# Where the update's weight chunks are split: GpSimd's early share ends four chunks sooner

## The reference

```python
def _L0_gnn_ref(n_f, ...):
    feat = jnp.concatenate([n_f[edge_src], n_f[edge_dst]], axis=1)
    e_hh = relu(feat[:E_HH] @ W_hh + b_hh)          # 128 edges
    e_oo = relu(feat[E_HH:E_HH + E_OO] @ W_oo + b_oo)   # 640 edges
    e_ho = relu(feat[E_HH + E_OO:] @ W_ho + b_ho)       # the rest
    logit = (concatenate([e_hh, e_oo, e_ho]) @ W_a + b_a)[:, 0]
    alpha = softmax of logit over the edges with the same edge_dst
    z_f = segment_sum(alpha[:, None] * n_f[edge_src], edge_dst)
    nf2 = jnp.concatenate([n_f, z_f], axis=1)
    h_new = relu(nf2[:64] @ W_hn + b_hn)
    o_new = relu(nf2[64:] @ W_on + b_on)
    return jnp.concatenate([h_new, o_new])
x = layernorm(x + L0(x, ...)); x = layernorm(x + L1(x, W, a, src, dst))
```

## Time and profile before

| what | value |
|---|---|
| three runs, median | 407.93 us (407.68 to 408.96) |
| profiled execution | 406.15 us |
| its span, first to last instruction | 404.2 us |
| mean granted TensorE clock | 0.924 |
| TensorE busy | 329.3 us, 81% of the span |
| VectorE, ScalarE, GpSimd busy | 303.8, 190.3, 142.5 us |

### The profile page before, as it was taken

One profiled execution on the slowest core, in us unless ns is written; L12 is line 12 of the kernel. 1 busy time (PEld: TensorE's weight loads), 2 busy tenths in 40 slices (PEclk: granted clock), 3 DMA queues, 4 the chain that ended last, 5 costly groups with the idle time before them and its releaser, 6 DMA issues.

```text
span 404.2 us, 4665 instructions
## 1 busy us (share of the span) xinstructions
PE 329.3 (81%) x1434; PEld 254.9 (63%) x1434; DVE 303.8 (75%) x398; ACT 190.3 (47%) x287; POOL 142.5 (35%) x202
## 2 busy tenths in 40 slices
PE   1889999991899769699999999972899990699480
PEld 1668888870355558488888888741688880588330
DVE  1599999933718958699999999898567689715635
ACT  3364585200302324786768777425246673323233
POOL 3200080460200710058988977392004332007000
PEclk9989999997799989899999999997799997589886
DMA  7995689799199955000300300333446982000002
GB/s 241 411 404 204 233 303 325 250 275 271 29 373 361 318 202 208 2 0 2 105 2 2 105 2 2 83 125 104 161 152 210 344 296 86 0 0 2 1 0 104
DMA packets 17639, 63.63 MB, mean 157 GB/s; under 512 B 2234, under 2 KB 2236, under 8 KB 17360
## 3 DMA queue, kind: packets, MB, share of 16 engines
q1 hardware_dynamic: 13520, 50.34, 34.2%
q0 software_dynamic: 2096, 8.74, 7.6%
q10 hardware_dynamic: 2000, 4.26, 3.2%
HBM read 60.16 MB, written 3.16 MB: 157 GB/s over the span
## 4 chain that ended last, share of the span: by engine, by line
PE 64%; DVE 19%; DMA 7%; ACT 4%; POOL 2%; issue 2%; DVEq 0%; ACTq 0%
PE ps L1163 19%; PE ps L1027 13%; PE ps L1049 9%; PE ps L1075 5%; PE ps L1194 5%; DMA last_rows<-table_scratch,st_col 4%; PE ps L1202 3%; DVE W_lo L655 3%; PE ps L1170 3%; POOL rows L365 2%; PE ps L1225 2%; DMA table_scratch<-tabs 2%; PE ps L1257 2%; DVE junk L811 2%; PE ps L1095 1%
## 5 line engine op out<-in xcount | busy, mean ns | idle before, releaser
L423 ACT CAST W_hi<-W_raw 128x1024 fp32r<-128x1024 f32 x72 | 73.3, 1047 | 57.7 <-PE ps L1027 28.7
L655 DVE TENSOR_TENSOR W_lo<-W_raw,W_hi 128x1024 fp32r<-128x1024 f32 x56 | 75.3, 1373 | 24.8 <-ACT W_hi L423 22.5
L865 DVE SCALAR_TENSOR_TENSOR ps<-ps,wa_bc 128x1024 f32<-128x1024 f32 x74 | 87.6, 1263 | 3.1 <-PE ps L1163 3.1
L354 POOL TENSOR_TENSOR W_lo<-W_raw,W_hi 128x1024 fp32r<-128x1024 f32 x16 | 39.4, 2474 | 81.3 <-ACT W_hi L423 81.3
L1163 PE MATMUL ps<-A_tab,oh 128*128 x148 | 53.9, 446 | 0.1
L1027 PE MATMUL ps<-W_hi,xT_hi 128*128 128x512 f32 x112 | 46.6, 416 | 7.9 <-DVE W_lo L655 7.9
L380 POOL TENSOR_SCALAR sc_r<-irow,keys 128x64 f32<-128x64 f32 x74 | 33.7, 455 | 45.4 <-PE ps L1170 45.1
L1163 PE MATMUL ps<-B_tab,oh 128*128 x148 | 47.2, 400 | 0.0
L1027 PE MATMUL ps<-W_lo,xT_hi 128*128 128x512 f32 x112 | 45.2, 403 | 0.0
L534 ACT ACTIVATE sc_l<-sc_l,keys 128x64 f32<-128x64 f32 x74 | 24.9, 341 | 24.5 <-DVE ps L865 18.3
L1027 PE MATMUL ps<-W_hi,xT_lo 128*128 128x512 f32 x112 | 35.4, 398 | 0.0
(11 more groups left out here) (216 smaller groups left out, 550.3 us busy)
## 6 DMA issues: line engine op xcount, KB each, us to landing
W_raw<-in_L_gnn_W_oo_dram SPq DMA_DIRECT2D x8, 1024.0 KB, 8.7
W_raw<-in_L_gnn_W_ho_dram SPq DMA_DIRECT2D x8, 1024.0 KB, 6.4
W_raw<-in_L_gnn_W_hh_dram SPq DMA_DIRECT2D x8, 1024.0 KB, 9.2
W_raw<-in_L_gnn_W_hn_dram SPq DMA_DIRECT2D x8, 1024.0 KB, 4.9
W_raw<-in_L_gnn_W_on_dram SPq DMA_DIRECT2D x8, 1024.0 KB, 5.1
W_raw<-in_L_gnn_W_dram SPq DMA_DIRECT2D x4, 1024.0 KB, 5.3
key_rows<-key_rows_scratch POOLq DMA_DIRECT2D x1, 2304.0 KB, 13.1
table_scratch<-tabs ACTq DMA_DIRECT2D x2, 1024.0 KB, 6.8
```

Source lines behind the costliest of these rows:

```text
L354: ga.tensor_tensor(W_lo[:, n % NB, :], W_raw[:, n // 2 % NS, n % 2, :], W_hi[:, n % NB, :].bitcast(F32), ALU.subtract).then_inc(lo_pool, 1)
L423: sa.copy(W_hi[:, n % NB, :], W_raw[:, n // 2 % NS, n % 2, :]).then_inc(hi_made, 1)
L655: v.tensor_tensor(W_lo[:, n % NB, :], W_raw[:, n // 2 % NS, n % 2, :], W_hi[:, n % NB, :].bitcast(F32), ALU.subtract).then_inc(lo_made, 1)
L865: v.scalar_tensor_tensor(acc, acc, 0.0, wa_bc[:], ALU.max, ALU.mult, accum_out=keys[:, t, 2:3]).then_inc(reduced, 1)
```

## The change

UX goes from 56 to 52. The diff is one line, but UX is used in `by_pool` and in the orders of three engines.

```diff
         END = {"ooA": 8, "ooB": 16, "hoA": 24, "hh": 40, "hoB": 48, "updx": 64, "upd": 80, "h1": 88}
 
-        UX = END["hoB"] + 2 * NB
+        UX = END["hoB"] + NB
 
         def by_pool(n):
```

## The result

The changed kernel takes 409.86 us (median of 14 runs, 407.73 to 411.42) where the kernel before takes 407.81 (14 runs, 406.0 to 409.37). The ratio is 1.0051, 95% interval 1.0029 to 1.0073: slower by 0.5%, some 2.1 us. The forecast was 408.7, no change that can be measured; the range held the time, and the case that came true is the second rival's.

The account below looks back on a forecast made before the run. VectorE's softmax chain, slowed by GpSimd's exclusion, bounds the weights, and TensorE the updates behind them. +6.47 - 3.74 - 1.96 = +0.77 us gives 408.7 us against a median of 407.93; range 406.7 to 410.8.

Parts of the forecast that it names:

- rival 2: TensorE's zT0 behind P: slower because the clock returns late; 411.0 if gone for all of zT0, midway 409.8; chance 0.24.
- P: Attention weights: P ready 5.70 us earlier, 3.74 from mean_logits and 1.96 from the scaling; transposes at 277.17 instead of 282.87.
- The collision of chunk 55: In mean_logits: GpSimd's one remaining subtraction, issued at about 265.8, blocks L813 or else L814; gain 3.74 instead of 5.78.
- The scaling: At L892: GpSimd has nothing then, so the second L892 takes 0.35 in place of 2.31; gain 1.96 us.
- rivals 4 and 5: Weights: chunk 55 blocks nothing, 406.7, chance 0.08; or GpSimd is not what slows them, 414.4, chance 0.03.
- Behind P: TensorE's node updates: four more chunks before the z half cost one period, 6.47 us, bounds 6.47 and 6.56.
- Rival 6: Updates behind P: the change adds nothing to that path, as updates overlap something else; -5.7, 402.2; chance 0.02.
- The clock: TensorE around the transposes and zT0: idle 12.7 us instead of 7.9, low at its end either way, difference priced at zero.
- The prediction's own sign for it: At zT0: the prediction is wrong if the low clock reaches past zT0's start by other than 3 us.
- the argument that stood against rival 2: On a late clock return at zT0: each execution of the kernel before had the same chance of it.
- The sum alone: Whole kernel: +6.47 behind P, -3.74 in mean_logits, -1.96 in the scaling, together +0.77 us, or +0.2%.

Follow-up runs that it names:

- GpSimd taking 52: The changed kernel, but GpSimd subtracts chunk 52 in place of 55 and VectorE 53 to 55; 407.34 us, 0.9989 of the kernel before.
- the order alone: The changed kernel's order of TensorE and ScalarE, but GpSimd still subtracts chunks 52 to 55; 413.27 us, 1.0120 of the kernel before.
- the clock full in both kernels: TensorE multiplies unread ones before P: 64 products in the changed kernel, 406.92 us; 136 in the kernel before, 406.46 us.
- the kernel before with 96 products: The kernel before, with TensorE doing 96 products of unread ones behind chunk 55 to keep its clock up; 407.12 us, ratio 0.9979.
- the version with VectorE's early subtractions: The kernel before (UX = 56), but GpSimd subtracts only 52, VectorE 53 to 55 behind mean_logits, ScalarE rounds 59 behind zT0; 402.46 us, ratio 0.9880.

## Why the prediction came out as it did

- *P.* Forecast 5.70 earlier, measured 5.72. The collision of chunk 55 fell as worked out: its subtraction was issued at 5.83 from the loop's end (5.9 forecast), L813 blocked for 2.45, L814 free. The scaling gained its 1.96. That GpSimd is the cause, rivals 4 and 5, is settled by GpSimd taking 52 (no block left, another 2.01 gained) and by the order alone (all blocks kept, 3.66 lost again).
- *Behind P.* Forecast 6.47, measured 6.45, with VectorE's three subtractions covered by zT0 (3.50 from 281.02, zT0 to 287.49), and SP's load of chunks 60 and 61 was issued when expected (283.40, 3.84 before the 287.24 of the earlier trace rows while the transposes moved by 3.85). Rival 6 falls.
- *The clock.* This is the step that failed: "so I price a difference of zero". The prediction's own sign for it came true, a low clock that reaches past the start of zT0 by other than 3 us. I took the moment of the return as evenly spread in both kernels, the argument that stood against rival 2. In the profile the low clock reached 5.7 us into zT0 in place of 3.0, at half speed 1.34 us. The transposes moved by 5.72 us and the return by 3.0. With the clock full in both kernels 0.73 us is left at the updates' end; as they are, 2.08. The term should have been about +1.3, the sum +2.1. It could not be read from the one trace of before, which shows a single return at this place; what could be read was that a shift of P by 5.7 us is no reason for the overlap to stay. The range held the time because its upper end was priced with nearly all of zT0 at the low clock.
- *The size of the effect against the 0.3%.* The sum alone, 0.2%, would have been no change. The clock's 1.3 us carried it past 0.3%, as rival 2 said it would from 0.9 us of delay on; the measured delay is 2.7 us.

The Trainium skill ("TensorE: Matmul & The Clock Gate", Part 1: The HAM clock gate) states that the monitor behind the clock runs freely and does not restart with a kernel. The runs agree in that the return does not follow the resumed work: with P as in the changed kernel and later by 1.46 and 2.91, it came at 24.9, 24.4 and 25.0. The Trainium skill says in the same section that the moment varies from run to run; here, against the loop's end, it lay within 0.6 us in these three kernels, and it lay 3.7 us earlier or 3.0 us and more later in others.

Open: each kernel has one profile, and that the low stretch has the same length in the unprofiled runs too is inferred from the medians (2.05 against the profile's 2.08) and from the mean clocks (0.905 to 0.913 in the 14 executions of the changed kernel). Why the return keeps to a few moments against the loop's end, and what picks one of them, was not tried. That earlier returns of the clock pull the work behind them into step would explain the first; that is argued, not shown.

## What to carry to other kernels

Where GpSimd and VectorE both work on a path that the end waits for, look for recorded durations that differ between two uses of one line: the excess is the block. Then ask which instruction beside it minds, since a reciprocal of 3.35 us is free cover for a GpSimd operation and a 0.43 us scalar operation costs 2.0. Moving TensorE's work from a stretch where it idles into one where it is the bound costs its whole duration; here it was better to free the other engine and leave the work there (0.9880 of the kernel before, against 1.0051). And where an edit moves the moment at which an idle TensorE resumes, price the low clock as an unknown of its own, between none and all of the first products behind it, in place of zero.

## What the runs showed of the hardware

- The granted clock fell inside work that had just resumed: 2.51 us of rest, the transposes of 0.66 and another 0.84 of rest came before it dropped at about 285.6 in the kernel before with 96 products (mean 0.80 over 285 to 286), and zT0 ran at the low level until 289.0. In the profile the same happened behind a gap of 1.64 us in the version with VectorE's early subtractions (zT0 5.41).
- GpSimd, issued 0.14 us before L812 ended (267.61 against 267.75), went ahead of L813, which followed 0.04 us after L812's end.
- 64 products of 128x128 ones took 3.75 us at the full clock, 5.29 us where the clock returned 3.3 us after their start (mean 0.63 over 274.5 to 275), and 6.53 us where it returned 5.8 us after it (0.90 over 276.5 to 277).
- The clock's returns inside zT0 fell into three groups against the loop's end, over eight kernels: 21.2; 24.4 to 25.0; 27.9 to 28.4 us.
